# A two-layer graph network on one core: VectorE's dependent small steps interleaved with a tile's passes, all four rho products of two tiles on GpSimd, and new tables

## The reference, cut to what matters

```
# layer 0, per block of 64 nodes
Wh = h @ W;  e = leaky(Whc @ a, 0.2)
scores = softmax(blocks * e, -1);  out = scores @ Whc
y = leaky(out @ W1 + b1); y = leaky(y @ W2 + b2); y = y @ W3 + b3
x = layernorm(x + layernorm(y + out) * ln_g + ln_b)
# layer 1, h has 4 heads of 32
scores = leaky_relu(s_left[i,h] + s_right[j,h] + adj[i,j] * we, 0.2)
scores += NEG where adj <= 1e-5
attn = softmax(scores, over j);  agg = attn @ h
x = layernorm(x + leaky_relu(x + agg + bias, 0.5))
```

## Time and profile before

| | |
|---|---|
| median of 3 runs | 2082.36 us (2081.89 to 2082.92) |
| the profiled execution | 2083.02 us, span 2081.1 us |
| busy: PE, DVE, ACT, POOL | 1853.0, 1888.0, 1565.1, 1842.9 us |
| first pass over a tile | VectorE's first L946 starts at 116.82 us |
| TensorE's mean granted clock | 0.963 of full |

### The profile page before, as it was taken

How to read it: one execution, slowest core, us unless ns; L and a number is a source line. 1 busy time by engine, 2 the same in 40 slices (tenths; PEclk the granted TensorE clock), 3 DMA queues, 4 the chain that set the end, 5 groups by cost and what they waited for, 6 DMA issues and landing times.

```text
span 2081.1 us, 34497 instructions
## 1 busy us (share of the span) xinstructions
PE 1853.0 (89%) x11304; PEld 918.9 (44%) x11304; DVE 1888.0 (91%) x3545; ACT 1565.1 (75%) x3448; POOL 1842.9 (89%) x664
## 2 busy tenths in 40 slices
PE   5789989999899998999898998989989999878886
PEld 4644444444444444444444444444444444433332
DVE  1279999999999999999999999999999999999997
ACT  6667887787877878788777887778787887666663
POOL 2079999999998999999999998999999998999995
PEclk8789999999999999999999999999999999999998
DMA  3232333323234232424233332332423422233320
GB/s 95 70 89 82 96 93 95 114 82 120 69 95 111 90 97 87 114 76 113 95 92 112 87 106 83 95 114 82 116 73 95 115 87 86 93 96 107 97 56 10
DMA packets 138617, 191.68 MB, mean 92 GB/s; under 512 B 22344, under 2 KB 56520, under 8 KB 138440
## 3 DMA queue, kind: packets, MB, share of 16 engines
q1 hardware_dynamic: 138440, 189.49, 31.2%
HBM read 180.82 MB, written 8.65 MB: 91 GB/s over the span
## 4 chain that ended last, share of the span: by engine, by line
PE 42%; DVE 22%; POOL 15%; issue 11%; ACT 8%; DVEq 1%; SPq 1%; DMA 0%; ACTq 0%; POOLq 0%
PE psum L1044 33%; POOL X L458 15%; DVE X L952 15%; PE psum L1201 7%; DVE X L946 3%; ACT E L714 2%; ACT psum L719 1%; ACT pen L677 1%; ACT x1s L615 1%; DVEq L862 1%; DVE x1s L885 1%; DVE est L861 1%; ACT o_sb L615 1%; PE psum L1162 1%; ACT blk L521 1%
## 5 line engine op out<-in xcount | busy, mean ns | idle before, releaser
L458 POOL TENSOR_TENSOR X<-RHO,E 128x1536 f32<-128x1536 f32 x512 | 1759.8, 3463 | 141.2 <-ACT E L714 134.0
L952 DVE SCALAR_TENSOR_TENSOR X<-psum,s_j,X 128x512 f32<-128x512 f32 x2048 | 1393.3, 745 | 51.9 <-POOL X L458 44.0
L1044 PE MATMUL psum<-X,haug 128*33 128x512 f32 x4096 | 1003.4, 611 | 4.7 <-DVE X L952 3.6
L714 ACT ACTIVATE E<-psum,we_s 128x512 f32<-128x512 f32 x512 | 397.6, 777 | 353.1 <-PE psum L1044 352.1
L1201 PE MATMUL psum<-ident,adj_sb 128*128 128x128 f32 x2048 | 439.0, 295 | 138.2 <-DVE X L952 134.1
L1201 PEld LDWEIGHTS psum<-ident,adj_sb 128*128 128x128 f32 x2048 | 290.5, 142 | 605.4 <-DVE X L952 410.2
L1044 PEld LDWEIGHTS psum<-X,haug 128*33 128x33 f32 x4096 | 198.5, 112 | 439.8 <-issue 402.6
L946 DVE TENSOR_TENSOR X<-psum,E 128x512 f32<-128x512 f32 x512 | 348.1, 680 | 44.6 <-ACT psum L521 43.3
L1044 PE MATMUL psum<-sgn_ident,pen 128*128 128x128 bf16 x2048 | 382.5, 222 | 0.0
L719 ACT ACTIVATE psum<-psum,we_s 128x512 f32<-128x512 f32 x512 | 381.1, 744 | 0.0
L677 ACT ACTIVATE pen<-adj_sb,pen_bias 128x512 bf16<-128x512 f32 x512 | 368.4, 720 | 1.1
(11 more groups left out here) (220 smaller groups left out, 1543.9 us busy)
## 6 DMA issues: line engine op xcount, KB each, us to landing
adj_sb<-in_adj_dram SPq DMA_DIRECT2D x128, 1024.0 KB, 5.2
RHO<-rho_scratch SPq DMA_DIRECT2D x32, 1024.0 KB, 9.6
out_dram<-o_sb SPq DMA_DIRECT2D x32, 256.0 KB, 2.8
xg<-in_x_dram SPq DMA_DIRECT2D x28, 256.0 KB, 5.7
blk<-in_adj_dram SPq DMA_DIRECT2D x56, 64.0 KB, 5.4
X<-in_x_dram SPq DMA_DIRECT2D x2, 256.0 KB, 3.1
W_sb<-in_L_gnn_W_dram SPq DMA_DIRECT2D x4, 64.0 KB, 2.0
X<-in_adj_dram SPq DMA_DIRECT2D x4, 64.0 KB, 3.0
```

The costliest lines, as they stand in the source:

```text
L458: Q.tensor_tensor(X[m % NX][:, 0:HP, :], RHO[:, g % 2, 0:HP, :], bc(E[m % NE][:], 1, [P, HP, GROUP]), ALU.mult).then_inc(B_pool, 1)
L714: A.activation(E[m % NE][:], TA[m % NT], ACT.Exp, scale=we_s[:, 3:4], bias=we_s[:, 5:6]).then_inc(E_sb, 1)
L952: ins = V.scalar_tensor_tensor(slot[:, h, :], TA[m % NT], s[:, k, h:h + 1], slot[:, h, :], ALU.mult, ALU.max)
L1044: return T.matmul(o, l, r, start=start, stop=stop)
```

## The change

`FOUR = (7, 35)`: in the tiles with these numbers GpSimd makes all four products (128x2048), and VectorE has no L946 (L1002 of the changed kernel). VectorE's small steps are cut into three parts. Part 0 stands ahead of the tile's product, part 1 behind the product, part 2 behind the first pass; in a tile of `FOUR` parts 1 and 2 stand behind the first and the second pass. The `link`s and the drain are gone: the later part waits for the earlier one's semaphore. After the last tile the parts stand one behind the other as before. The tables are new throughout; of the many places those that the prediction speaks of are in the diff.

```diff
+    FOUR = (7, 35)
-    AT_PE = {... "ST": (-10, 8, 20, 30), "oT": (-8, 9, 21, 32), "y1": (-7, 10, 22, 33), ...
-          "g0": (-2, 15, 27, 38), ... "x1T": (9, 25, 41, 48), "h0": (10, 27, 43, 49) ...}
+    AT_PE = {... "ST": (-11, 7, 20, 29), "oT": (-10, 10, 21, 32), "y1": (-9, 11, 22, 33), ...
+          "g0": (-4, 16, 27, 37), ... "x1T": (6, 26, 41, 48), "h0": (7, 27, 43, 49) ...}
-    AT_DVE = {"max": (-17, -12, 10, 24), "rin": (-14, -10, 13, 26), "res": (1, 18, 30, 41),
-          "r_stats": (3, 19, 33, 41)}
-    AT_POOL = {"xb": (-19, -11, 12, 24), "r_shift": (7, 23, 35, 45)}
+    AT_DVE = {"max": (-20, -9, 10, 25), "rin": (-16, -8, 13, 27), "res": (0, 19, 30, 41), "r_stats": (2, 20, 33, 42)}
+    AT_POOL = {"xb": (-24, -8, 20, 27), "r_shift": (5, 23, 37, 45)}
-    ONCE_PE = {"rmT": 52, "Rb": 53, "rhoT": 56, "hsum": 57}
-    ONCE_DVE = {"rm": 53, "R4": 54, "lam": 56}
+    ONCE_PE = {"rmT": 52, "Rb": 53, "rhoT": 56, "hsum": 58}
+    ONCE_DVE = {"rm": 52, "R4": 54, "lam": 55}
-    EPI_DVE = {"part0": 4, "part1": 5, "stats": 7}
+    EPI_DVE = {"part0": 3, "part1": 5, "stats": 7}
...
+        def own(m):
+            return m % BODY not in FOUR
...
             def tile(m):          # GpSimd
...
-                Q.tensor_tensor(X[m % NX][:, 0:HP, :], RHO[:, g % 2, 0:HP, :],
-                                bc(E[m % NE][:], 1, [P, HP, GROUP]), ALU.mult).then_inc(B_pool, 1)
+                heads = HP if own(m) else H
+                Q.tensor_tensor(X[m % NX][:, 0:heads, :], RHO[:, g % 2, 0:heads, :],
+                                bc(E[m % NE][:], 1, [P, heads, GROUP]), ALU.mult).then_inc(B_pool, 1)
...
-            def stats(st, mean_var, src, done):
+            def moments(st, src, done):
                 for t in range(GT):
-                    V.bn_stats(st[:, t, :], src(t))
-                dve.drain()
+                    ins = V.bn_stats(st[:, t, :], src(t))
+                ins.then_inc(done, 1)
+
+            def mean_var(st, out, ready, count, done):
+                dve.wait_ge(ready, count)
                 for t in range(GT):
-                    V.bn_aggr(mean_var[:, t, :], st[:, t, :]).then_inc(done, 1)
+                    V.bn_aggr(out[:, t, :], st[:, t, :]).then_inc(done, 1)
...
-            def epi_part(g, r):
+            def epi_rden(g, r):
                 dve.wait_ge(nat_ps, 2 * g + r + 1)
...
-                link(V.reciprocal(rden[:, r], parts[:, :, :, DH]))
-                link(V.tensor_tensor(parts[:, :, :, 0:DH], parts[:, :, :, 0:DH], ...))
-                V.tensor_tensor(sums[:, r], parts[:, :, :, 0:DH], own[:, r], ALU.add).then_inc(res_sb, 1)
+                V.reciprocal(rden[:, r], parts()[:, :, :, DH]).then_inc(rden_sb, 1)
+
+            def epi_scale(g, r):
+                dve.wait_ge(rden_sb, 2 * g + r + 1)
+                V.tensor_tensor(parts()[:, :, :, 0:DH], parts()[:, :, :, 0:DH], ...).then_inc(scaled, 1)
+
+            def epi_add(g, r):
+                dve.wait_ge(scaled, 2 * g + r + 1)
...
             def tile(m):          # VectorE
...
+                epilogue(m, 0)
+                host(m, 0)
+                if own(m):
...
+                    V.tensor_tensor(slot[:, HP, :], RB, E[m % NE][:], ALU.mult).then_inc(B_dve, 1)
+                    epilogue(m, 1)
+                    host(m, 1)
...
                 for h in range(H):
...
                     ins = V.scalar_tensor_tensor(slot[:, h, :], TA[m % NT], s[:, k, h:h + 1], slot[:, h, :],
                                                  ALU.mult, ALU.max)
...
+                    part = h + 1 if not own(m) else h + 2
+                    if part <= 2:
+                        epilogue(m, part)
+                        host(m, part)
```

More of the change, by code:

```diff
@@ L209, in prev, with owned @@
             return c - 2
+        def own(m):
+            return m % BODY not in FOUR
+        def owned(m):
+            full, n = divmod(m, BODY)
+            return full * (BODY - len(FOUR)) + n - sum(1 for f in FOUR if f < n)
         def uses(c):
@@ L275, in build_program @@
         act_step = sem("act_step")
-        dve_step = sem("dve_step")
+        raw_ps = sem("raw_ps")
+        st_r = sem("st_r")
+        est = sem("est")
+        rden_sb = sem("rden_sb")
+        scaled = sem("scaled")
         acc_zero = sem("acc_zero")
@@ L1010, in _ @@
             for c in U:
-                r_stats(c)
+                r_moments(c)
+            for c in U:
+                r_var(c)
             for c in (NB, NB + 1):
@@ L1017, in _ @@
             make_R4(0)
+            make_raw(0)
             make_lam(0)
```

142 lines of the change are left out of this document (82 added, 60 removed), and 6 rows, old and new, of the table AT_PE.

## The result

The changed kernel takes 2029.24 us (median of 4 runs, 2025.75 to 2030.75) against 2082.12 (2081.67 to 2082.92): 52.9 us less, ratio 0.9745 (0.9732 to 0.9759). The forecast was 2054, with a range of 2038 to 2082, so the sign was right, and the size and the range were wrong: the gain is nearly twice the 28 us of the sum. Its profiled execution took 2030.75 us.

The account below looks back on a forecast made before the run. No engine bounds the whole: VectorE and TensorE alternate by stretch, with none full in the sixth. Stretch terms summed to -3.5 us a batch, -28.0 in eight, from 2083.0 to 2055.0, so a median of 2054; range 2038 to 2082.

Parts of the forecast that it names:

- What bounds each stretch: Third batch in eight stretches: VectorE full in first, third, fifth, seventh; TensorE in second, fourth, eighth; nobody in sixth.
- GpSimd takes over from TensorE: Eighth stretch: GpSimd becomes the full engine, needing 32.9 us where it needed 31.7 before; +1.3 us a batch.
- That makes 3.7 us a batch: VectorE's stalls: eight parts 1.84, four epilogue statistics 1.04, four `r_stats` 0.60, two more pairs of 0.12; bounds 0 and 5.
- Sixth: full of waits, no engine relieved: 0: Sixth stretch of a batch: no engine full, so no change in its length.
- the seventh's -0.4: Seventh stretch, VectorE's: 0.46 + 0.26 saved, `make_lam` (0.5) comes in, a reciprocal and other pieces go; -0.4 us a batch.
- where unit 3's residual and statistics shared a tile: One of two extra dependent pairs on VectorE, counted as 0.12 us a batch saved.
- The rival of a step that the tables place badly: A table's step comes too early: 32 x 0.5 = 16 us given back, 2070 us; chance 0.10.
- the wait at k = 3: Reciprocal one tile sooner, waiting for TensorE's first back-projection, 0.5 us a group; such a new wait would refute the forecast.
- Full relief: Rival: two of three clock drops a batch vanish as TensorE's waits shorten, 14 us less than forecast, 2041; chance 0.15.
- that TensorE has its idle time elsewhere then: Second stretch: with 2.3 us less to do there, TensorE idles elsewhere; held against the rival of vanishing clock drops.
- The products: Tiles 7 and 35: VectorE saves 0.59 us each; GpSimd pays 1.15 each, hidden at tile 7 but not at 35.
- VectorE waits 1.1 us: Tile 35: VectorE's first pass waits for GpSimd's larger product, giving back the saving and half a microsecond more.

Follow-up runs that it names:

- e_s: Changed kernel with the old tables and no four-product tiles, so only the small steps are split: 2037.49 us, 0.9784 of the kernel before.
- e_fix: e_st with unit 0's ST, oT, y1, y2 one tile later on TensorE and ScalarE, and z on TensorE: 2024.30 us, 0.9719 of the kernel before.
- e_haug: e_st with GpSimd's four haug products at tiles 59, 62, 66 and 69 instead of 59 to 62: 2032.48 us, 0.9770 of the kernel before.
- e_contig: e_s with all parts of a step issued together ahead of the tile's product, semaphores kept: 2081.83 us, 1.0006 of the kernel before.
- e_r42: Kernel before with one table number changed, r_stats of unit 3 at tile 42 instead of 41: 2064.15 us, 0.9922 of the kernel before.
- e_warm: Kernel before with three more zero-weight matmuls in tiles 6, 40 and 53 of each batch: 2073.23 us, 0.9961 of the kernel before.
- e_st: Changed kernel without four-product tiles (split steps and new tables): 2024.16 us, 0.9722 of the kernel before.

## Why the prediction was wrong

**What bounds each stretch** was read rightly for the first five: where VectorE was full its steps counted nearly in full (`e_s`), and the fourth stretch did not move. The eighth got longer by 3.2 us a batch, 2.1 without the residual that is only moved, where the sum had 1.3. That GpSimd takes over from TensorE there was wrong: TensorE is busy for 33.00 of its 33.00 us, and GpSimd for 31.08, and relieving either alone (`e_fix`, `e_haug`) gained nothing.

**"That makes 3.7 us a batch"** is the first step that failed, a term mis-sized. A part saved 4.27 - 3.97 = 0.30 us, not 0.23; epilogue statistics 5.17 - 4.86 = 0.31, not 0.26; `r_stats` 4.45 - 4.27 = 0.18, not 0.15, and the tile with `make_lam` 0.14, not 0.12. With the counts of the prediction that is 8 x 0.30 + 4 x 0.31 + 4 x 0.18 + 0.14 = 4.5. The working compared a dependent pair with an independent one, which is right, but took the distances of the independent ones a little too long: reciprocal and scaling are followed after 0.11 and 0.33, not 0.12 and 0.35, the sum after 0.33, not 0.34, and the product, which now stands behind the short reciprocal, after 0.56, not 0.59. The sum of the four distances is 0.24 + 0.46 + 0.34 + 0.59 = 1.63 by the earlier trace rows, and 0.11 + 0.56 + 0.33 + 0.33 = 1.33 above (the first pass's own distance left out). `e_s` and `e_contig` show that the split alone, without tables or products, is the larger part, 6.1 us a batch. Only 4.5 of them are steps; the other 1.6 are the next point.

**"Sixth: full of waits, no engine relieved: 0"** is the step that failed outright, with the seventh's -0.4 beside it. Measured -2.6 and -2.3. A stretch full of waits has a cause ahead of it, and the cause was in the stretch: two steps of the chain in one tile of VectorE's, a wait of 2.04 us on TensorE, a clock drop in most batches, and TensorE late through tiles 42 to 46. The drop alone is worth 1.6 us there. The new tables move `r_stats` of unit 3 to 42, as `e_r42` does. The prediction's own text named this ("where unit 3's residual and statistics shared a tile") and gave it 0.12 us. One number of the kernel before brought 17 us. The rival of a step that the tables place badly (0.10) was there as well, at a place that the prediction had not looked at, `hsum`; it costs nothing as long as TensorE is late behind tile 53 anyway. So was its own example, the wait at k = 3, with 0.65 us a batch.

**Full relief** had 0.15 and was in its mechanism nearly right. Drops of the clock went from 2 or 3 in each of the batches two to seven to one. Most lie behind TensorE's waits for a long tile of VectorE's, so a shorter one can save twice; `e_warm`, and the two batches of before without the drop at tile 42, show that the drops were on the path. The split alone made TensorE's wait for passes fall from 134.1 to 96.3 us in all, in these rows of the groups of the kernel before and of `e_s`:

```profile
L1201 PE MATMUL psum<-ident,adj_sb 128*128 128x128 f32 x2048 | 439.0, 295 | 138.2 <-DVE X L952 134.1 <-issue 3.7
```

```profile
L1266 PE MATMUL psum<-ident,adj_sb 128*128 128x128 f32 x2048 | 435.0, 293 | 100.7 <-DVE X L1013 96.3 <-issue 3.4
```

The argument held against it, that TensorE has its idle time elsewhere then, was wrong: the second stretch has no drop any more. The measured time lies below its 2041, as VectorE's term was larger too.

**The products** came out near nothing, and by another way than forecast. GpSimd's 1.08 us lay just below the bounds of 1.09 to 1.21. "VectorE waits 1.1 us" at tile 35 was wrong: VectorE's wait was 0.3, because with the new tables GpSimd is further ahead at that place than the 0.5 us of the earlier trace rows said: 1.7 us in `e_st`, 0.3 in `e_s`. The tables of before have GpSimd's small shift of unit 2 in tile 35, just ahead of the product, where it waited 0.48 us for ScalarE; the new ones have it at 37, and the prediction took the lead from the old place. What tile 35 saved went back at tile 37, and most of the 0.56 us of tile 7 in tiles 14, 15 and 57. GpSimd has little slack left, which fits: its busy share of the third batch is 231.7 of 238.7 us. The prediction called itself wrong at over 95% with VectorE waiting for more than 100 us; the first came, the second did not (46.3).

**The sum** by what was measured: a batch 4.5 for the steps, 1.6 for waits and clock that go with them (`e_s`: 6.1 in all), and 2.1 more for tables and products, makes 8.2 a batch. Over the whole, from first product to first product, six batches (two to seven) gave 51.1 us together, and the last with the end 4.1, while the start took 2.7 longer and the first batch, which now ends behind a residual, 0.2. That is the 52.4 us between the two spans.
